# A two-layer convolution block: residual by chunks, a shorter far path, group means with a signed matrix, and a new order in the second layer

## What is computed

```
# layer 0: deformable sampling, 8 heads of 8 channels, 9 taps (k)
v       = Wv @ gn(x)
offsets = conv3x3(gn(x), off_w) + off_b        # dx, dy per head, tap and pixel
aw      = sigmoid(conv3x3(gn(x), attn_w) + attn_b)
out     = Wo @ sum over k of aw[k] * bilinear(v, pixel + offsets[k])
# layer 1
p1, p2  = relu(conv3x3(gn(x), p1_w) + p1_b), relu(conv3x3(gn(x), p2_w) + p2_b)
pooled  = cummax of p1 upwards in y + cummax of p2 leftwards in x
a       = group_norm(conv3x3(pooled, p_w)) * g + b
c       = group_norm(conv1x1(gn(x), c1_w)) * g1 + b1
out     = relu(conv3x3(relu(a + c), c2_w) + c2_b)
```

## Time and profile before

| | |
|---|---|
| median of 3 runs | 163.49 us (161.29, 163.49, 163.99) |
| the profiled execution | 164.37 us, of which the profile's span is 162.5 us |
| PE, PE weight loads | 130.0 us busy (80%), 110.9 us (68%) |
| DVE | 112.7 us busy (69%) |
| ACT, POOL | 59.2 us (36%), 22.4 us (14%) |
| TensorE's granted clock | mean 0.964 of full |

### The profile page before, as it was taken

The page is one execution under the profiler, slowest core; times in us unless marked ns, Lnnn a source line. Parts: engine busy times, 40 slices in busy tenths (PEclk is TensorE's granted clock), DMA queues, the critical chain, the costliest instruction groups (busy, mean ns, idle before and its releaser), DMA issues.

```text
span 162.5 us, 3252 instructions
## 1 busy us (share of the span) xinstructions
PE 130.0 (80%) x1387; PEld 110.9 (68%) x1387; DVE 112.7 (69%) x195; ACT 59.2 (36%) x107; POOL 22.4 (14%) x27
## 2 busy tenths in 40 slices
PE   0069109999899899999999998998689996685790
PEld 0057009999799789999899886886476564453560
DVE  5515997059148999699969999985580596857611
ACT  3009058660990469007962054020010415103301
POOL 8817900000000000000035000000010101020100
PEclk9999955999999999999999999999978999999998
DMA  4991000009963000000000000000000000000014
GB/s 127 246 188 28 0 0 0 4 0 257 237 128 78 0 2 4 0 0 4 0 0 0 4 0 0 0 0 6 2 0 4 0 6 4 0 4 0 0 36 97
DMA packets 7058, 5.96 MB, mean 37 GB/s; under 512 B 4656, under 2 KB 6194, under 8 KB 7042
## 3 DMA queue, kind: packets, MB, share of 16 engines
q1 hardware_dynamic: 6370, 4.71, 12.6%
q10 hardware_dynamic: 672, 1.02, 2.5%
HBM read 3.31 MB, written 0.52 MB: 24 GB/s over the span
## 4 chain that ended last, share of the span: by engine, by line
PE 48%; DVE 26%; issue 10%; DMA 7%; ACT 5%; SPq 1%; POOL 1%; POOLq 0%; DVEq 0%
PE bank L964 9%; PE bank L979 9%; PE bank L1004 7%; PE bank L958 7%; DMA x_t<-in_x 7%; DVE prod L733 6%; PE bank L924 4%; DVE part L760 3%; DVE x_t L859 3%; PE bank L1095 3%; PE bank L1128 3%; PE bank L939 2%; DVE wy L768 2%; DVE g_t L702 2%; DVE pooled L865 1%
## 5 line engine op out<-in xcount | busy, mean ns | idle before, releaser
L760 DVE TENSOR_TENSOR part<-v,bank 128x1280 f32<-128x1280 f32 (+3 forms) x20 | 21.5, 1111 | 9.7 <-PE bank L1004 4.3
L733 DVE TENSOR_TENSOR prod<-hat,wy 128x1440 f32<-128x1440 f32 (+3 forms) x25 | 27.3, 1158 | 0.0
L979 PE MATMUL bank<-cst,prod 128*128 128x128 f32 (+3 forms) x189 | 22.3, 272 | 0.8 <-DVE prod L733 0.8
L979 PEld LDWEIGHTS bank<-cst,prod 128*128 128x128 f32 (+3 forms) x189 | 20.7, 132 | 1.4 <-DVE prod L733 1.0
L1004 PE MATMUL bank<-cst,part 128*128 128x128 f32 x168 | 20.9, 274 | 0.8 <-issue 0.4
L924 PE MATMUL bank<-ones_r 128*128 128x512 f32 x71 | 20.8, 452 | 0.0
L958 PE MATMUL bank<-w_pair,g_pair 128*128 128x216 f32 x96 | 15.0, 294 | 7.0 <-ACT w_pair L432 7.0
L1004 PEld LDWEIGHTS bank<-cst,part 128*128 128x128 f32 x168 | 18.3, 140 | 2.1 <-DVE part L760 1.8
L964 PE MATMUL bank<-w_cross,g_cross 128*128 128x216 f32 x144 | 19.6, 283 | 0.0
L964 PEld LDWEIGHTS bank<-w_cross,g_cross 128*128 128x128 f32 x144 | 18.3, 201 | 0.0
L958 PEld LDWEIGHTS bank<-w_pair,g_pair 128*128 128x128 f32 x96 | 12.8, 202 | 7.7 <-ACT w_pair L432 7.4
(11 more groups left out here) (91 smaller groups left out, 166.5 us busy)
## 6 DMA issues: line engine op xcount, KB each, us to landing
v<-v SPq DMA_DIRECT2D x2, 480.0 KB, 6.3
v<-v SPq DMA_DIRECT2D x2, 448.0 KB, 5.8
x_t<-in_x SPq DMA_DIRECT2D x1, 512.0 KB, 10.9
prod<-in_w_off ACTq DMA_DIRECT2D x1, 486.0 KB, 7.5
prod<-in_w_off SPq DMA_DIRECT2D x1, 486.0 KB, 9.7
w_s<-in_w SPq DMA_DIRECT2D x4, 72.0 KB, 3.7
wc_s<-in_wc SPq DMA_DIRECT2D x2, 144.0 KB, 3.0
wp_s<-in_wp SPq DMA_DIRECT2D x4, 72.0 KB, 2.9
```

Source lines behind the costliest of these rows:

```text
L733: return nc.vector.tensor_tensor(prod[:, 0:K2 * CELLS * cx].rearrange("p (k q s) -> p q k s", k=K2, s=cx)[:, q0:q0 + nd], hat[:, c % 2, d0 ...
L760: nc.vector.tensor_tensor(part[:, n % PARTS, 0:nd, 0:cv].rearrange("p d (q e) -> p d q e", e=HD), moved, weights.unsqueeze(3).to_broadcast ...
L979: last = nc.tensor.matmul(out_ps[0:size, b * P:(b + 1) * P], prod[:, at:at + size], ident, start=(b == 0 and t == 0), stop=(b == n - 1 and ...
```

## The change

- **Residual chunk by chunk.** `residual(c)` adds the columns of a chunk for all images. `residual(c - 1)` stands in chunk c on DVE, ahead of the fourth `apply`; only `residual(4)` stands behind the last chunk. `x1` gets memory of its own, since it is now written while the convolution's tiles are in use.
- **Far path.** One double loop over all rows and columns in place of five pieces; it adds into `x1` instead of `x_b`.
- **Group means.** Beside the averaging matrix `C_GB` there is a signed one, `C_GD`, which gives half the difference of the two channels' means. The variance of the group is the mean of the variances plus the square of that, so L591 and L592 go for all but layer 0's normalisation, and PE makes two matmuls for a group mean. The constants grow from 543 to 671 columns.
- **Inputs of layer 1.** DVE alone makes `g1`, as (x - mean) * rstd, without an affine step. `WARM_IN` is (5, 4, 4), and both group means of the input stand ahead of `branch_conv(0)`.
- **Order in layer 1.** On ACT both `branches` stand ahead of both `affine_c`; on DVE `pools(1)` stands ahead of `c1_stats(1)`; PE's group means move from `pool_conv(0)` into `pool_conv(1)`.
- **End.** ACT prepares `x1_b` = x1 + bias early; DVE makes the result in one step from PSUM, max(o, -bias) + x1_b. Images 0 and 2 are stored by SP and images 1 and 3 by ACT, both halves each.

```diff
-WARM_IN = (11, 14)
+WARM_IN = (5, 4, 4)
...
+    c[:, C_GD:C_GD + P] = c[:, C_GB:C_GB + P] * np.where(i[:, None] == i[None, :], 1, -1)
...
@@ scalar @@
-            act.wait_ge(borders, 1)
-            for g in range(2):
-                n = DUO * g
-                act.wait_ge(norm_ready, G_IN + g + 1)
-                nc.scalar.activation(inner(g1, n, 1)[:, 0], rows_cols(x1[:, n, :]), ACT.Identity,
-                                     bias=ab[:, G_IN + g, 3, 0:1],
-                                     scale=ab[:, G_IN + g, 2, 0:1]).then_inc(g1_ready, 1)
...
+            act.wait_ge(x1_ready, 1)
+            nc.scalar.activation(x1_b, x1[:, :, :], ACT.Identity, bias=vec_s[:, 4:5]).then_inc(x1_b_ready, 1)
             branches(0)
+            branches(1)
             affine_c(0)
-            branches(1)
+            affine_c(1)
             second_input(0)
-            affine_c(1)
             second_input(1)
-            outputs(0)
-            outputs(1)
-            for n in range(HALF):
+            for n in range(1, HALF, 2):
                 act.wait_ge(res_ready, n + 1)
-                act.dma_start(out_d[HALF + n], res[hi, n, :]).then_inc(stored, 16)
+                for half, rows in enumerate((lo, hi)):
+                    act.dma_start(out_d[n, half], res[rows, n, :]).then_inc(stored, 16)
@@ vector @@
+            def pair_variance(s):
+
+                ve.wait_ge(stats_ps, s + 1)
+                means, apart = pair_stats(s)[:, 0:2 * DUO].rearrange("p (n t) -> p t n", t=2), pair_stats(s)[:, 2 * DUO:]
+                link(nc.vector.tensor_copy(sq[:, s, 0:DUO], apart))
+                link(nc.vector.tensor_tensor(sq[:, s, 0:DUO], apart, sq[:, s, 0:DUO], ALU.mult))
+                nc.vector.scalar_tensor_tensor(ab[:, s, 1, 0:DUO], means[:, 1], EPS, sq[:, s, 0:DUO],
+                                               ALU.add, ALU.add).then_inc(var_ready, 1)
+                link(nc.vector.tensor_copy(ab[:, s, 0, 0:DUO], means[:, 0]))
...
+                ROW, CELL = 5, 8
+                per_row = ROW + FULL * CELL
...
-                for r0, r1, ranges in FAR_ROWS:
-                    per_row = 5 + sum(i1 - i0 for i0, i1 in ranges) * CELL
-                    with ve.Fori(r0, r1) as k:
-                        base = n + (k - r0) * per_row
-                        ve.wait_ge(far_v, (k + 1) * 16)
-                        base = run(base, row_steps(k))
-                        for i0, i1 in ranges:
-                            base = columns(base, i0, i1)
-                        ve.sem_inc(far_row_done, 1)
-                    n += per_row * (r1 - r0)
+                with ve.Fori(0, FULL) as k:
+                    ve.wait_ge(far_v, (k + 1) * 16)
+                    base = run(first + k * per_row, row_steps(k))
+                    with ve.Fori(0, FULL) as i:
+                        run(base + i * CELL, cell_steps(i))
+                    ve.sem_inc(far_row_done, 1)
...
+            def add_input(par, j0, j1):
+
+                def columns(t):
+                    return t[:, :, :].rearrange("p n (y j a) -> p a j y n", a=2, j=W // 2)[:, par, j0:j1]
+                return nc.vector.tensor_tensor(columns(x1), y0_banks[par][:, :].rearrange(
+                    "p (j y n) -> p j y n", y=H, n=HALF)[:, j0:j1], columns(x_b), ALU.add)
+
+            def residual(c):
+
+                x0, w = CHUNKS[c]
+                ve.wait_ge(y0_ps, c + 1)
+                for par in range(2):
+                    last = add_input(par, x0 // 2, (x0 + w) // 2)
+                return last
...
-                for i in APPLY[:-1]:
+                for m, i in enumerate(APPLY[:-1]):
+                    if c and m == ND - 2:
+                        residual(c - 1)
                     apply(i)
...
+                for j in range(DUO):
+                    n = DUO * g + j
+                    nc.vector.tensor_scalar(inner(g1, n, 1)[:, 0], rows_cols(x1[:, n, :]), ab[:, s, 0, j:j + 1],
+                                            ab[:, s, 2, j:j + 1], ALU.subtract, ALU.mult).then_inc(g1_ready, 1)
...
+            x1_stats(0)
+            pair_variance(G_IN)
+            x1_stats(1)
             ve.wait_ge(borders, 1)
             first_input(0)
-            x1_stats(1, added)
-            variance(G_IN + 1, DUO, pair_stats(G_IN + 1))
-            affine(G_IN + 1, DUO)
+            pair_variance(G_IN + 1)
             first_input(1)
...
+            def results(g):
+                ve.wait_ge(o_ps, g + 1)
+                for k in range(DUO):
+                    n = DUO * g + k
+                    nc.vector.scalar_tensor_tensor(res[:, n, :], pair_banks(OUT_BANK[g])[:, k], neg_b[:, 0:1],
+                                                   x1_b[:, n, :], ALU.max, ALU.add).then_inc(res_ready, 1)
+
             c1_stats(0)
             pools(0)
-            c1_norm(0)
+            pair_variance(G_C1)
+            c1_affine(0)
+            pools(1)
             c1_stats(1)
-            pools(1)
-            c1_norm(1)
             p_stats(0)
+            pair_variance(G_C1 + 1)
+            pair_variance(G_P)
+            c1_affine(1)
             both_branches(0)
             p_stats(1)
+            pair_variance(G_P + 1)
             both_branches(1)
...
@@ tensor @@
+            def group_mean(s):
+
+                pe.wait_ge(stats_in, s + 1)
+                stat = pair_stats(s)
+                nc.tensor.matmul(stat[:, 0:2 * DUO], cst[:, C_GB:C_GB + P],
+                                 mv[:, s, 0:DUO, :].rearrange("p n t -> p (n t)"), start=True, stop=True)
+                nc.tensor.matmul(stat[:, 2 * DUO:], cst[:, C_GD:C_GD + P], mv[:, s, 0:DUO, 0], start=True,
+                                 stop=True).then_inc(stats_ps, 1)
...
             keep_warm(WARM_IN[0], bank[0][:, :])
-            group_means(G_IN, DUO, pair_stats(G_IN), (C_GB,))
+            group_mean(G_IN)
             keep_warm(WARM_IN[1], bank[0][:, :])
+            group_mean(G_IN + 1)
+            keep_warm(WARM_IN[2], bank[0][:, :])
...
-                branch_conv(g, {6: G_IN + 1} if g == 0 else {4: G_C1})
+                branch_conv(g, {4: G_C1} if g else {})
                 skip_conv(g)
-            pool_conv(0, {4: G_C1 + 1})
-            pool_conv(1, {6: G_P})
+            pool_conv(0, {})
+            pool_conv(1, {2: G_C1 + 1, 4: G_P})
```

More of the change, by code:

```diff
@@ L190, in build @@
         u_flat = u[:, :, :, :].rearrange("p k x h -> p (k x h)")
-        res = u_flat[:, 0:HALF * HW].rearrange("p (n q) -> p n q", q=HW)
+        res, x1_b = (u_flat[:, i * HALF * HW:(i + 1) * HALF * HW].rearrange("p (n q) -> p n q", q=HW)
+                     for i in range(2))
         psum = ctx.enter_context(nc.psum_tensor("bank", [P, 8, 512], F32))
@@ L275, in build @@
         x_d = x.rearrange("n c h w -> n c (h w)")
-        out_d = out.rearrange("n c h w -> n c (h w)")
+        out_d = out.rearrange("(a n) c h w -> n a c (h w)", a=2)
         lo, hi = slice(0, C), slice(C, P)
@@ L354, in _ @@
                                  v_dram[bass.ds(k * N, P), :]).then_inc(far_v, 16)
-            for n in range(HALF):
+            for n in range(0, HALF, 2):
                 sp.wait_ge(res_ready, n + 1)
-                sp.dma_start(out_d[n], res[lo, n, :]).then_inc(stored, 16)
+                for half, rows in enumerate((lo, hi)):
+                    sp.dma_start(out_d[n, half], res[rows, n, :]).then_inc(stored, 16)
             sp.wait_ge(stored, 2 * 16 * HALF)
@@ L549, in second_input @@
                                      bias=ab[:, G_P + g, 3, 0:1]).then_inc(g2_ready, 1)
-            def outputs(g):
-                act.wait_ge(o_ps, g + 1)
-                for k in range(DUO):
-                    nc.scalar.activation(res[:, DUO * g + k, :], pair_banks(OUT_BANK[g])[:, k], ACT.Relu,
-                                         bias=vec_s[:, 4:5]).then_inc(relu_ready, 1)
             act.wait_ge(ld_vec, 32)
+            act.wait_ge(x1_ready, 1)
+            nc.scalar.activation(x1_b, x1[:, :, :], ACT.Identity, bias=vec_s[:, 4:5]).then_inc(x1_b_ready, 1)
             branches(0)
+            branches(1)
             affine_c(0)
-            branches(1)
+            affine_c(1)
             second_input(0)
-            affine_c(1)
             second_input(1)
-            outputs(0)
-            outputs(1)
-            for n in range(HALF):
+            for n in range(1, HALF, 2):
                 act.wait_ge(res_ready, n + 1)
-                act.dma_start(out_d[HALF + n], res[hi, n, :]).then_inc(stored, 16)
+                for half, rows in enumerate((lo, hi)):
+                    act.dma_start(out_d[n, half], res[rows, n, :]).then_inc(stored, 16)
         @block.vector
@@ L809, in _, with x1_stats @@
                 far_displacements()
-            ve.wait_ge(y0_ps, NC)
-            def residual(g):
-                n0 = DUO * g
-                for par in range(2):
-                    def column_pairs(t):
```

(33 more changed lines are left out.)

64 lines of the change are left out of this document (25 added, 39 removed).

## The result

The kernel after takes 158.27 us (median of 4 runs, 157.51 to 158.58) beside 163.41 (161.29 to 163.99): a ratio of 0.971, with a 95% interval of 0.967 to 0.975. The prediction said 157.9, with a range of 155.8 to 160.5. The profiled execution took 158.49 us, 156.7 of it span, where the sum had 158.7.

The account below looks back on a forecast made before the run. No engine is full; a chain of waits changing engines sets the end. Terms 3.9 + 0.3 + 2.3 + 0.5 - 0.15 + 0.3 - 1.2 - 0.3 = 5.65 take the profiled 164.37 to 158.7, median 163.49 to 157.9; range 155.8 to 160.5.

Parts of the forecast that it names:

- Stages 3, 4 and 6: PE's pool_conv(0) to pool_conv(1), gain 2.3 us; from there to out_conv(0), gain 0.5; out_conv(1) to the end, gain 0.3.
- Stages 2 and 5: PE's branch_conv(0) to pool_conv(0), gain 0.3 us; out_conv(0) to out_conv(1), loss 0.15.
- The price of the long code: DVE's branch over the far path before the last residual: skipping 52 instructions instead of 271 gains 1.8 us.
- a fetch: At DVE's branch over the far path, idle time was read as the target being fetched; 1.8 us of gain.
- the restart with the projection: Sign: DVE's idle time ahead of the last residual ends with the projection; before, DVE began 1.8 us after it.
- the gap without a packet: Sign: no instruction packet lies in DVE's idle time before the last residual; before, one of 8 KB did.
- Stage 1: From layer 0's last projection to branch_conv(0) on PE: 10.03 us before, 6.1 after, gain 3.9.
- PE starts the branches late because of its own warming: Between the layers, 14 warm matmuls fill 118.49 to 123.54 us, though the first pair was normalised soon after 121.
- The base of the sum: The whole kernel's profiled execution, 164.37 us, 0.9 above the median of 163.49; stage durations were taken from it.
- The clock rival: Between the layers, PE's clock falls with halved warming, costing 1.7 us on branch_conv(0): 159.6 us; chance 0.2.
- The chunks' loss: Residual additions inside layer 0's chunks: 0.7 us in the fourth and 0.5 in the last, loss 1.2.
- The head's: At the kernel's start, 66 KB more constants queue ahead of `x_t`: loss 0.3 us.

## Why the prediction was right, and where its reasons were not

- **Stages 3, 4 and 6** were right by mechanism and to 0.15 us, from durations of single rows and the new order. The order of `pools(1)` and ACT's `branches(1)` must both be changed for stage 3; undone singly they cost 0.92 and 1.94 of start. (ACT's branches(1) can start 0.49 ahead of pool_conv(0), 133.38 to 133.87 in the kernel before; the 0.66 is the skip convolution's duration. Nothing hangs on it.) No run undoes the new end, or DVE's making `g1` alone: their worth is read off the stages only.
- **Stages 2 and 5** were right to 0.25 and 0.15. In stage 2 the price of the group mean that goes was too low: branch_conv(0) takes 4.04 without it (121.21 to 125.25) and took 4.52 with it, 0.48 for 0.3. In stage 5 the second matmul costs 0.23 and DVE's steps 0.06, where 0.15 was taken.
- **The price of the long code** was right: shortening what the branch skips from 271 to 52 instructions took away 1.78 us of DVE's idle time in one kernel, and putting it back gave 1.77 in the other. Its cause, a fetch, is argued: of its two signs, the restart with the projection came, and the gap without a packet did not in the kernel before with the short far path. The Trainium skill's rule (Runtime: NRT & Kernel Launch, Instruction fetch mechanics), that a taken branch to a target outside the held blocks stalls, agrees with the idle time. Its block size, 256 instructions, neither explains the stall nor excludes it, since no row shows where in a block the branch stands; the packets are of 8 KB, half of its block.
- **Stage 1's number was right and its reading wrong.** The step "PE starts the branches late because of its own warming" failed: with 4 matmuls in place of 14 the kernel before got 0.7% slower. The 14 kept the clock up, or took the low clock on themselves, over a wait of 1.70 that came from DVE's late restart; with the short far path 10 of them can go. The terms of the sum held because the change shortens the far path and the warming together.
- **The base of the sum** was an execution with the fall of the clock. About 1.6 of stage 1's 3.9 is this fall, which 26 of 42 other executions of the kernel before don't have; in them the stage gains some 2.5 (10.03 less 1.6, to 5.92), of which 1.8 is the restart of DVE. The forecast hardly depends on it: their median of 162.66 less the sum's other 4.05 is 158.6, as near to the 158.27 measured as 157.9 is. So the fall changes what stage 1 is said to be worth, and not the time.
- **The clock rival** had the right place and price for one fall (1.7; measured 1.7 to 2.0 on branch_conv(0)), but it was set as a risk of halved warming. In the kernel after, where the clock stays full, no wait of PE exceeds 1.1 us in layer 1 and 0.74 between the layers. Each experiment that made one of these waits 1.6 or longer brought the clock down.
- **The chunks' loss** of 1.2 was 1.08 (0.56 and 0.52), and the run with all additions at the end confirms it. **The head's** 0.3 for the constants was 0; the 0.77 there is the clock of that execution. With 0.3 in the sum and 0.77 in the trace, the stages gained 0.5 more than the sum, and the two met: luck in the profiled span.

## What to carry to other kernels

Price an edit that shortens or lengthens a wait of PE by the convolution behind it too: here each of four orders whose own cost is 1 to 2 us cost 3 to 5, since the clock fell. And see first whether the execution that was profiled is like the others: a mean clock of 0.964 beside 0.979 in most showed here that it wasn't. Matmuls that look like a delay may be covering such a fall; look at the granted clock under them before taking them out, and at what made PE wait. And code that is never run can cost time: here 1.8 us with 271 instructions to skip instead of 52.

## What was not expected of the hardware

- PE's clock fell to 0.50 in or behind waits of 1.70, 1.60 (with one of 1.58 soon after), 1.62, 1.99, 2.03, 2.27 and 3.02 us. It did not behind 1.48 and 1.58, nor behind 1.82 in the earlier trace rows ahead of out_conv(0), and not in most executions of the kernel before, whose profile has the 1.70. The wait alone doesn't settle it. The Trainium skill (TensorE: Matmul & The Clock Gate, HAM oscillation) describes bursts whose waits bring the clock down; these runs show it at waits of 1.6 to 3.0.
- A low clock costs matmuls that use a part of the array (64 rows, 64 or 32 columns each) near the full factor: 40 of pool_conv took 4.54 for 2.39.
- The low stretch that begins while PE waits for the first inputs, at 20 to 24 us, begins and ends at a time of its own in each execution, and with it the same code reached the last projection between 114.41 and 116.22. That is 1.8 us, where the four times of the kernel after spread by 1.1.
